# Last mixing of a four-layer spectral kernel in units of a quarter of the rows, round the four column groups

## Chip, cores and metric

One core of a Trainium2 chip runs the whole program. The metric is the device time of one execution in microseconds.

## What is computed

The input x is 16 images of 32 channels, 64 by 64, in float32. Four layers follow each other, each of the form x + layer(group norm of x). The change concerns the fourth, a full spectral convolution, and the place where its weights' spectra are made and kept:

```python
def _L3_conv_ref(x, weights):              # weights: (32, 32, 64, 64)
    x_f = jnp.fft.rfft2(x)
    k_f = jnp.fft.rfft2(weights)
    out_f = jnp.einsum('bchw,ochw->bohw', x_f, k_f)
    return jnp.fft.irfft2(out_f, s=(H, W))
```

For each frequency the einsum mixes 32 input channels into 32 output channels: a complex 32x32 product applied to 16 images.

## The kernel before

`kernel_spectra_stage` runs first. For each of 8 tiles of the fourth layer's weights, PE transposes and multiplies (L378 to L417), DVE and ACT empty the banks, and ACT gathers the spectra of a tile in `ks_spec` (L352, eight copies) and stores them with two DMAs from its own queue (L357) in the DRAM tensor `kf`. Before the first copy of the next tile, ACT waits until they have landed (`stored`). The other layers follow. The first one has a mixing of its own (`l0_mix_stage`, L762): 448 matmuls with 64 rows by 32 weight columns and 32 moving columns, whose neighbours lie in different column groups and alternate between two halves of the rows; it is not in a hardware loop. In the second layer, L1048 and L1082 are a subtraction (on POOL and DVE in turn) and a cast on DVE.

In the fourth layer the forward transform leaves the spectrum of x in `xm`: 128 partitions are four groups of 32 channels, one group for each quarter of the frequencies of a slot; the free axis is slot (8), frequency (64), real or imaginary, image (16). `l3_mix_stage` multiplies by the weights' spectra and writes the result back over `xm`, and `inverse_stage` (L840 on) goes back to pixels and adds.

A complex product is one real matmul here. Its contraction axis has 128 rows: for two slots (`s2`) 32 real and 32 imaginary channels each. The stationary side are 128x32 of `m_kf`, the moving side 64 columns of `m_xp`. For these, three copies on DVE stage each quadrant of 32 partitions: the spectrum as it is into the real rows (L1513), and into the imaginary rows the real part (L1514) and the negated imaginary part (L1515), the turned spectrum. A result of 32 rows lies in one of the four column groups of a bank. A float32 matmul stands as two records in the trace.

The order of the work is written out by hand. The loops run over four pairs of slots `i`, two pairs of groups `p`, two halves of the frequencies `half`, the two groups `j` of the pair, and 32 frequencies `m`. So 32 matmuls in a row lie in the same column group (L1561); after 64, `mixed` is raised. DVE stages the next half but one as soon as `mixed` frees its `m_xp`; SP loads the spectra of a pair of groups (2 MB, four DMAs of 512 KB in 8 KB runs, each to 32 partitions, L1475) as soon as `m_kf` is free; ACT empties four banks on 64 partitions (L1577) after each half. POOL only zeroes one of two `m_xp` at the start (L1542, L1543).

```python
for m in range(H):
    at = (2 * p + j) * C
    last = pe.matmul(ps[4 * half + m // 8][at:at + C, m % 8 * N:(m % 8 + 1) * N],
                     kf[p][:, j, :, H * half + m],
                     xp[half][:, j, m].rearrange("p s n -> p (s n)"), ...)
```

## Time and profile before

| | |
|---|---|
| device time, median of 3 runs | 1067.43 us (1066.34 to 1069.4) |
| span of the profiled execution | 1065.9 us |
| PE busy | 907.4 us (85%) |
| DVE, ACT, POOL busy | 663.4, 520.5, 122.4 us |
| mixing matmuls, L1561 | 116.5 us busy, 2048 records |
| granted PE clock, mean | 0.948 |

The span runs from the first to the last instruction of one profiled execution; that execution's own device time is not listed apart from the runs, whose lowest lies 0.4 us above the span and whose median 1.5 us. A group of the profile gives the busy time, the mean of one instruction, and the idle time in front of it with what ended it. Idle time of an engine that is waited for by nobody costs nothing.

### The profile page before, as it was taken

Reading aid. Unit: us, or ns where it says so; the run is one execution under the profiler, and the core shown is the slowest. Engines: PE = TensorE matmul, PEld = TensorE weight load, DVE = VectorE, ACT = ScalarE, POOL = GpSimd, SP = SyncE. Lnnn points to the kernel's source line nnn. Section 1 sums busy time; section 2 is a strip of 40 time slices with the busy share of each in tenths; the row PEclk is TensorE's granted clock in tenths of the full one; section 3 lists DMA queues with packets and bytes.
Section 4 is the critical chain, followed back from the end, with each engine's and each line's share of the span. In section 5 each row is a group of like instructions: output and inputs, shape, how many; then the busy total and the mean of one; then the engine's idle time right before and its main releaser. Section 6 shows DMA issues by size and latency. Waiting matters only on the chain. (4 is left out here: it accounts for less than half of the span.)

```text
span 1065.9 us, 25662 instructions
## 1 busy us (share of the span) xinstructions
PE 907.4 (85%) x9335; PEld 764.7 (72%) x9335; DVE 663.4 (62%) x1208; ACT 520.5 (49%) x900; POOL 122.4 (11%) x120
## 2 busy tenths in 40 slices
PE   6999999876449956599789999995888699998998
PEld 6999999765348843499644444443887699998998
DVE  3556463765584769578778565756666688881232
ACT  2444444575344436255369997000888423225554
POOL 0000000010001016155401223000000100001110
PEclk9999999898679989699999999997999899999999
DMA  6465766464300000000000000001300337750222
GB/s 249 159 243 195 272 216 202 129 147 94 76 4 1 0 14 1 0 1 0 0 2 1 0 0 0 0 0 29 66 0 0 79 82 146 145 103 1 89 108 118
DMA packets 47673, 79.12 MB, mean 74 GB/s; under 512 B 19322, under 2 KB 37888, under 8 KB 44816
## 3 DMA queue, kind: packets, MB, share of 16 engines
q1 hardware_dynamic: 30992, 61.80, 20.9%
q10 hardware_dynamic: 16640, 16.78, 4.5%
q8 instruction: 26, 0.43, 0.2%
q14 instruction: 15, 0.12, 0.0%
HBM read 50.65 MB, written 27.92 MB: 74 GB/s over the span
## 5 line engine op out<-in xcount | busy, mean ns | idle before, releaser
L1436 DVE SCALAR_TENSOR_TENSOR X<-bank,c_power,X 32x512 f32 x128 | 95.8, 748 | 58.8 <-PE bank L1404 53.6
L1561 PE MATMUL bank<-m_xp,m_kf 128*32 128x64 f32 x2048 | 116.5, 224 | 6.8 <-DVE m_xp L1529 5.4
L1561 PEld LDWEIGHTS bank<-m_xp,m_kf 128*32 128x32 f32 x2048 | 116.2, 139 | 7.2 <-issue 7.2
L1404 PE MATMUL bank<-c_rh,c_w_high 128*128 x288 | 110.3, 383 | 3.3 <-DVE c_rl L1349 3.3
L1404 PE MATMUL bank<-c_rl,c_w_high 128*128 x288 | 110.2, 383 | 0.0
L1404 PE MATMUL bank<-c_rh,c_w_low 128*128 x288 | 110.2, 383 | 0.0
L923 DVE TENSOR_TENSOR X<-X,bank 128x512 f32 x64 | 43.6, 682 | 91.6 <-PE bank L909 91.6
L204 DVE BATCH_NORM_STATS2 bn<-X 128x6 f32 x128 | 85.6, 684 | 2.4 <-POOL X L1208 1.6
L1577 ACT COPY xm<-bank 64x512 f32 x64 | 32.5, 584 | 95.4 <-PE bank L1561 95.4
L1363 ACT ACTIVATE c_r<-X,c_nrm 32x1024 f32 (+1 forms) x56 | 73.6, 1314 | 2.4 <-DVE c_nrm L1412 1.1
L438 DVE COPY ks_cols<-bank 128x512 f32<-128x512 f32 x64 | 42.6, 682 | 45.9 <-PE bank L404 45.9
L435 DVE COPY ks_tt<-bank 128x512 f32<-128x512 f32 x64 | 42.3, 688 | 44.1 <-PE bank L378 44.1
L352 ACT COPY ks_spec<-bank 128x512 f32<-128x512 f32 x64 | 37.4, 587 | 65.4 <-PE bank L412 29.1
L1161 PE MATMUL bank<-mm,p_tt 128*128 128x128 f32 x512 | 63.0, 278 | 3.1 <-DVE X L1191 3.1
L385 PE MATMUL bank<-ks_fw,ks_tt 128*128 128x128 f32 x512 | 64.6, 277 | 0.0
L412 PE MATMUL bank<-ks_fh,ks_cols 128*128 128x128 f32 x512 | 63.7, 275 | 0.0
L1161 PEld LDWEIGHTS bank<-mm,p_tt 128*128 128x128 f32 x512 | 59.9, 193 | 4.8 <-DVE X L1191 4.5
L385 PEld LDWEIGHTS bank<-ks_fw,ks_tt 128*128 128x128 f32 x512 | 61.3, 194 | 0.0
L447 ACT COPY ks_src<-bank 128x512 f32<-128x512 f32 x64 | 37.2, 587 | 48.4 <-PE bank L385 48.4
L412 PEld LDWEIGHTS bank<-ks_fh,ks_cols 128*128 128x128 f32 x512 | 60.4, 192 | 0.0
L909 PE MATMUL bank<-c_l_iw,i_tt 128*128 128x128 f32 (+1 forms) x384 | 60.1, 310 | 0.0
L626 DVE TENSOR_TENSOR f_tl<-bank,f_th 128x512 f16<-128x512 f32 x64 | 42.3, 683 | 26.1 <-ACT f_th L581 25.9
(187 smaller groups left out, 1951.7 us busy)
## 6 DMA issues: line engine op xcount, KB each, us to landing
ks_src<-in_L_conv_weights SPq DMA_DIRECT2D x32, 512.0 KB, 6.3
kf<-ks_spec ACTq DMA_DIRECT2D x16, 1024.0 KB, 10.0
m_kf<-kf SPq DMA_DIRECT2D x32, 512.0 KB, 8.0
X<-in_x SPq DMA_DIRECT2D x4, 2048.0 KB, 12.3
out_y<-X SPq DMA_DIRECT2D x16, 512.0 KB, 2.7
xf<-f_xm SPq DMA_DIRECT2D x6, 448.0 KB
l_wb<-in_L_conv_weights_r SPq DMA_DIRECT2D x4, 512.0 KB, 13.1
l_wb<-in_L_conv_weights_i SPq DMA_DIRECT2D x4, 512.0 KB, 14.7
```

The source lines that it names most:

```text
L204: dve.bn_stats(self.bn[:, c, :], self.X[:, q, c * CH:(c + 1) * CH]).then_inc(step, 1)
L385: m = pe.matmul(ps[4 + j % 4][:, k * P:(k + 1) * P], tt[j % 4][:, k * P:(k + 1) * P], fw[:], start=True, stop=True)
L412: m = pe.matmul(ps[4 + s % 4][:, b * P:(b + 1) * P], cols[:, b, 4 * s:4 * s + 4].rearrange("p s c -> p (s c)"), fh[:], start=True, stop=True)
L435: dve.tensor_copy(tt[j % 4][:], ps[j % 4][:]).then_inc(turned_read, 1)
L438: dve.tensor_copy(cols[:, :, 4 * s:4 * s + 4].rearrange("p b s c -> p s b c"), ps[s % 4][:].rearrange("p (s b c) -> p s b c", s=4, b=IB)). ...
L909: m = pe.matmul(ps[4 + c % 4][:, k * n:(k + 1) * n], tt[g % 4][:, (first + k) * P:(first + k + 1) * P], mw[:], start=True, stop=True)
L923: dve.tensor_tensor(x, x, ps[4 + c % 4][:], ALU.add).then_inc(added, 1)
L1161: m = pe.matmul(ps[2 + 2 * (j % 2) + t][:, k * P:(k + 1) * P], tt[j % 2][:, k * P:(k + 1) * P], mm[:, t, :], start=True, stop=True)
L1363: act.activation(to, of, ACT.Identity, scale=nrm[at, 0, bass.ds(q, 1)], bias=nrm[at, 1, bass.ds(q, 1)]).then_inc(ready[b], 1)
L1404: m = pe.matmul(ps[n][:], w[:, ky, kx].rearrange("p o c -> p (o c)"), d[:, q, b, y:y + HALF, x:x + HN], start=i == 0, stop=i == len(terms) ...
L1436: dve.scalar_tensor_tensor(x, ps[n][o * C:(o + 1) * C, :].rearrange("p (y x) -> p y x", x=HN), filt.power[at, 2:3], x, ALU.mult, ALU.add). ...
L1561: last = pe.matmul(ps[4 * half + m // 8][at:at + C, m % 8 * N:(m % 8 + 1) * N], kf[p][:, j, :, H * half + m], xp[half][:, j, m].rearrange( ...
```

## The change

The mixing goes in four units of 16 frequencies a pair of slots, and within a unit through all four column groups for each frequency. `m_xp` holds four groups of 16 frequencies instead of two of 32. The spectra of the weights lie in DRAM by halves of the frequencies, so that one load brings all four groups of one half: as before 2 MB, in runs of 4 KB; the stores of a tile become four DMAs with runs of 512 bytes. Staging is divided: POOL writes the turned spectrum of a unit, for all 128 partitions at once, into a new tile `m_turned` (one subtraction from zero, one copy); DVE copies the eight quadrants of the spectrum and three of the turned one into `m_xp`, ACT the other five. ACT empties two banks on 128 partitions a unit, one unit behind its staging. PE waits for both stagers (`staged`), POOL for both before it writes over `m_turned`, the stagers for `swapped` of POOL and for `mixed` of two units before. In the first pair, where the real frequencies at the edge are packed, small extras of POOL and DVE replace the fix-up copies.

```diff
-        self.kf = nc.dram_tensor("kf", (SLOT // 4, P, 2, C // IB, IB * N), F32, kind="Internal").ap()
+        self.kf = nc.dram_tensor("kf", (SLOT // 4, P, 2, 2, C // IB, IB * HN), F32, kind="Internal").ap()
...
-        spec = pr.sb(ctx, "ks_spec", [P, SLOT // 4, 2, IB, N])
+        spec = pr.sb(ctx, "ks_spec", [P, SLOT // 4, 2, 2, IB, HN])
...
                             if s == 0:
-                                act.wait_ge(stored, START + 64 * i + 32 * p)
-                            act.copy(spec[:, s].rearrange("p r o k -> p o r k"),
-                                     ps[4 + s % 4][:].rearrange("p (o r k) -> p o r k", o=IB, r=2)
+                                act.wait_ge(stored, START + 128 * i + 64 * p)
+                            act.copy(spec[:, s].rearrange("p r h o k -> p o (r h) k"),
+                                     ps[4 + s % 4][:].rearrange("p (o r k) -> p o r k", o=IB, r=4)
                                      ).then_inc(made_read, 1)
                         act.wait_ge(made_read, START + base + 16)
-                        for part in range(2):
-                            act.dma_start(pr.kf[:, :, part, 2 * i + p, :].rearrange("s p n -> p s n"),
-                                          spec[:, :, part].rearrange("p s o k -> p s (o k)")).then_inc(stored, 16)
+                        for part, half in np.ndindex(2, 2):
+                            act.dma_start(pr.kf[:, :, part, half, 2 * i + p, :].rearrange("s p n -> p s n"),
+                                          spec[:, :, part, half].rearrange("p s o k -> p s (o k)")).then_inc(stored, 16)
...
-def load_kernel_spectra(sp, pr, to, i, pair, loaded):
+def load_kernel_spectra(sp, pr, to, i, half, loaded):
     for s2 in range(2):
         for part in range(2):
             at = (2 * s2 + part) * C
-            sp.dma_start(to[at:at + C].rearrange("c j o k -> c j (o k)"),
-                         pr.kf[2 * i + s2, pair * 2 * C:(pair + 1) * 2 * C, part].rearrange(
-                             "(j c) t n -> c j (t n)", j=2)).then_inc(loaded, 16)
+            sp.dma_start(to[at:at + C].rearrange("c g o k -> c g (o k)"),
+                         pr.kf[2 * i + s2, :, part, half].rearrange("(g c) t n -> c g (t n)", g=4)).then_inc(loaded, 16)
...
-    staged, mixed, mixed_read, fix, zeroed = (pr.sem(f"m3_{n}") for n in
-                                              ("staged", "mixed", "mixed_read", "fix", "zeroed"))
-    H = N // 2
+    UNITS = 4
+    H, U = N // 2, N // 4
+    staged = {n: pr.sem(f"m3_staged_{n}") for n in ("dve", "act")}
+    mixed, mixed_read, fix, zeroed, cleared, swapped = (pr.sem(f"m3_{n}") for n in
+                                               ("mixed", "mixed_read", "fix", "zeroed", "cleared", "swapped"))
     with ExitStack() as ctx:
-        kf = [kf0, pr.sb(ctx, "m3_kf1", [P, 2, C, N])]
-        xp = [pr.sb(ctx, f"m3_xp{p}", [P, 2, H, 2, 2 * B]) for p in range(2)]
+        kf = [kf0, pr.sb(ctx, "m3_kf1", [P, 4, C, H])]
+        xp = [pr.sb(ctx, f"m3_xp{p}", [P, 4, U, 2, 2 * B]) for p in range(2)]
+        turned = [pr.sb(ctx, f"m3_turned{p}", [P, 2, U, 2 * B]) for p in range(2)]
+        nought = pr.zero[:].unsqueeze(2).unsqueeze(3).broadcast_to([P, 2, U, B])
+        def spectrum(i, u):
+            return xm[:, bass.ds(2 * i, 2), U * u:U * u + U]
+        def copy_real(copy, i, u, only):
+            for g, s2 in only:
+                last = copy(xp[u % 2][2 * s2 * C:(2 * s2 + 1) * C, g, :, s2],
+                            xm[g * C:(g + 1) * C, 2 * i + s2, U * u:U * u + U].rearrange("p k r b -> p k (r b)"))
+            return last
+        def copy_imaginary(copy, u, only):
+            for g, s2 in only:
+                last = copy(xp[u % 2][(2 * s2 + 1) * C:(2 * s2 + 2) * C, g, :, s2],
+                            turned[u % 2][g * C:(g + 1) * C, s2])
+            return last
+        quadrants = [(g, s2) for g in range(4) for s2 in range(2)]
         with nc.Block() as block:
             @block.sync
             def _(sp):
                 load_kernel_spectra(sp, pr, kf[1], 0, 1, loaded[1])
                 with sp.Fori(1, PAIRS) as i:
-                    for p in range(2):
-                        sp.wait_ge(mixed, START + 4 * i + 2 * p - 2)
-                        load_kernel_spectra(sp, pr, kf[p], i, p, loaded[p])
-            def stage(dve, i, p, half, quadrants=(0, 1)):
-                for j in quadrants:
-                    for s2 in range(2):
-                        of = xm[(2 * p + j) * C:(2 * p + j + 1) * C, 2 * i + s2, H * half:H * half + H]
-                        re = xp[half][2 * s2 * C:(2 * s2 + 1) * C, j, :, s2]
-                        im = xp[half][(2 * s2 + 1) * C:(2 * s2 + 2) * C, j, :, s2]
-                        dve.tensor_copy(re, of.rearrange("p k r b -> p k (r b)"))
-                        dve.tensor_copy(im[:, :, B:2 * B], of[:, :, 0, :])
-                        last = dve.tensor_scalar(im[:, :, 0:B], of[:, :, 1, :], -1.0, None, ALU.mult)
-                return last
+                    for half in range(2):
+                        sp.wait_ge(mixed, START + UNITS * i + 2 * half - 2)
+                        load_kernel_spectra(sp, pr, kf[half], i, half, loaded[half])
+            @block.gpsimd
+            def _(pool):
+                pool.memset(xp[1][0:2 * C, :, :, 1], 0.0).then_inc(cleared, 1)
+                pool.memset(xp[1][2 * C:P, :, :, 0], 0.0).then_inc(cleared, 1)
+                pool.wait_ge(cleared, 2)
+                def turn(i, u, done):
+                    of, to = spectrum(i, u), turned[u % 2]
+                    pool.tensor_tensor(to[:, :, :, 0:B], nought, of[:, :, :, 1, :], ALU.subtract)
+                    pool.tensor_copy(to[:, :, :, B:2 * B], of[:, :, :, 0, :]).then_inc(done, 1)
+                for u in range(UNITS):
+                    if u >= 2:
+                        pool.wait_ge(staged["dve"], u - 1)
+                        pool.wait_ge(staged["act"], u - 1)
+                    turn(0, u, swapped if u % 2 else cleared)
+                    if u % 2 == 0:
+                        pool.wait_ge(cleared, u // 2 + 3)
+                        pool.memset(turned[0][0:C, 0, 0, 0:B], 0.0)
+                        pool.tensor_copy(turned[0][0:C, 0, 0, B:2 * B], xm[0:C, 0, U * u, 1, :]).then_inc(swapped, 1)
+                with pool.Fori(1, PAIRS) as i:
+                    for u in range(UNITS):
+                        pool.wait_ge(staged["dve"], UNITS * i + u - 1)
+                        pool.wait_ge(staged["act"], UNITS * i + u - 1)
+                        turn(i, u, swapped)
             @block.vector
             def _(dve):
-                for half in range(2):
-                    if half == 1:
-                        dve.memset(xp[1][0:2 * C, :, :, 1], 0.0)
-                        dve.memset(xp[1][2 * C:P, :, :, 0], 0.0)
-                    stage(dve, 0, 0, half, (0,)).then_inc(fix, 1)
-                    dve.wait_ge(fix, 3 * half + 1)
-                    dve.memset(xp[half][0:C, 0, 0, 0, B:2 * B], 0.0).then_inc(fix, 1)
-                    dve.memset(xp[half][C:2 * C, 0, 0, 0, 0:B], 0.0).then_inc(fix, 1)
-                    dve.tensor_copy(xp[half][C:2 * C, 0, 0, 0, B:2 * B], xm[0:C, 0, H * half, 1, :]).then_inc(staged, 1)
-                    stage(dve, 0, 0, half, (1,)).then_inc(staged, 1)
-                for half in range(2):
-                    dve.wait_ge(mixed, START + half + 1)
-                    stage(dve, 0, 1, half).then_inc(staged, 2)
+                dve.memset(xp[0][0:2 * C, :, :, 1], 0.0).then_inc(zeroed, 1)
+                dve.memset(xp[0][2 * C:P, :, :, 0], 0.0).then_inc(zeroed, 1)
+                dve.wait_ge(zeroed, 2)
+                dve.wait_ge(cleared, 2)
+                def stage(i, u, first=False):
+                    last = copy_real(dve.tensor_copy, i, u, quadrants)
+                    if first and u % 2 == 0:
+                        last.then_inc(fix, 1)
+                        dve.wait_ge(fix, u // 2 + 1)
+                        dve.memset(xp[0][0:C, 0, 0, 0, B:2 * B], 0.0)
+                    dve.wait_ge(swapped, UNITS * i + u + 1)
+                    copy_imaginary(dve.tensor_copy, u, quadrants[5:]).then_inc(staged["dve"], 1)
+                for u in range(UNITS):
+                    if u >= 2:
+                        dve.wait_ge(mixed, START + u - 1)
+                    stage(0, u, True)
                 with dve.Fori(1, PAIRS) as i:
-                    for p in range(2):
-                        for half in range(2):
-                            dve.wait_ge(mixed, START + 4 * i + 2 * p + half - 1)
-                            stage(dve, i, p, half).then_inc(staged, 2)
-            @block.gpsimd
-            def _(pool):
-                pool.memset(xp[0][0:2 * C, :, :, 1], 0.0).then_inc(zeroed, 1)
-                pool.memset(xp[0][2 * C:P, :, :, 0], 0.0).then_inc(zeroed, 1)
+                    for u in range(UNITS):
+                        dve.wait_ge(mixed, START + UNITS * i + u - 1)
+                        stage(i, u)
             @block.tensor
             def _(pe):
                 pe.sem_inc(mixed, START)
                 pr.keep_warm(pe, 16)
-                pe.wait_ge(zeroed, 2)
                 with pe.Fori(0, PAIRS) as i:
-                    for p in range(2):
-                        pe.wait_ge(loaded[p], 64 * i + 64)
-                        for half in range(2):
-                            pe.wait_ge(mixed_read, START + 4 * i + 2 * p + half - 1)
-                            for j in range(2):
-                                pe.wait_ge(staged, 8 * i + 4 * p + 2 * half + j + 1)
-                                pe.sem_inc(pr.pace, 1)
-                                for m in range(H):
-                                    at = (2 * p + j) * C
-                                    last = pe.matmul(ps[4 * half + m // 8][at:at + C, m % 8 * N:(m % 8 + 1) * N],
-                                                     kf[p][:, j, :, H * half + m],
-                                                     xp[half][:, j, m].rearrange("p s n -> p (s n)"),
-                                                     start=True, stop=True)
-                            last.then_inc(mixed, 1)
+                    for u in range(UNITS):
+                        half = u // 2
+                        if u % 2 == 0:
+                            pe.wait_ge(loaded[half], 64 * i + 64)
+                        for n in ("dve", "act"):
+                            pe.wait_ge(staged[n], UNITS * i + u + 1)
+                        pe.wait_ge(mixed_read, START + UNITS * i + u - 3)
+                        pe.sem_inc(pr.pace, 1)
+                        for m in range(U):
+                            for g in range(4):
+                                last = pe.matmul(ps[2 * u + m // 8][g * C:(g + 1) * C, m % 8 * N:(m % 8 + 1) * N],
+                                                 kf[half][:, g, :, U * (u % 2) + m],
+                                                 xp[u % 2][:, g, m].rearrange("p s n -> p (s n)"),
+                                                 start=True, stop=True)
+                        last.then_inc(mixed, 1)
             @block.scalar
             def _(act):
                 act.sem_inc(mixed_read, START)
-                with act.Fori(0, PAIRS) as i:
-                    for p in range(2):
-                        for half in range(2):
-                            act.wait_ge(mixed, START + 4 * i + 2 * p + half + 1)
-                            for m in range(4):
-                                at = slice(p * 2 * C, (p + 1) * 2 * C)
-                                k = H * half + 8 * m
-                                c = act.copy(xm[at, bass.ds(2 * i, 2), k:k + 8].rearrange("p s k r b -> p k s (r b)"),
-                                             ps[4 * half + m][at, :].rearrange("p (k s n) -> p k s n", s=2, n=2 * B))
-                            c.then_inc(mixed_read, 1)
+                def read(i, u):
+                    act.wait_ge(mixed, START + UNITS * i + u + 1)
+                    for m in range(2):
+                        k = U * u + 8 * m
+                        c = act.copy(xm[:, bass.ds(2 * i, 2), k:k + 8].rearrange("p s k r b -> p k s (r b)"),
+                                     ps[2 * u + m][:].rearrange("p (k s n) -> p k s n", s=2, n=2 * B))
+                    c.then_inc(mixed_read, 1)
+                def stage(i, u):
+                    act.wait_ge(swapped, UNITS * i + u + 1)
+                    copy_imaginary(act.copy, u, quadrants[:5]).then_inc(staged["act"], 1)
+                act.wait_ge(zeroed, 2)
+                act.wait_ge(cleared, 2)
+                for u in range(UNITS):
+                    if u >= 2:
+                        act.wait_ge(mixed, START + u - 1)
+                    stage(0, u)
+                    if u:
+                        read(0, u - 1)
+                with act.Fori(1, PAIRS) as i:
+                    for u in range(UNITS):
+                        act.wait_ge(mixed, START + UNITS * i + u - 1)
+                        stage(i, u)
+                        if u:
+                            read(i, u - 1)
+                        else:
+                            read(i - 1, UNITS - 1)
+                read(PAIRS - 1, UNITS - 1)
...
-                kf0 = pr.sb(inner, "m3_kf0", [P, 2, C, N])
+                kf0 = pr.sb(inner, "m3_kf0", [P, 4, C, HN])
```

What this does to the order on PE. Before, in a pair of slots (the loop's first half):

```order
L1555 ISA
L1557 ISA
L1561 MATMUL bank<-m_xp,m_kf 32x64 x32
L1557 REGISTER_ALU
L1561 MATMUL bank<-m_xp,m_kf 32x64 x32
```

and now, one unit and the start of the next:

```order
L1596 ISA
L1598 REGISTER_ALU
L1602 MATMUL bank<-m_xp,m_kf 32x64 x64
L1596 REGISTER_ALU
L1598 REGISTER_ALU
L1602 MATMUL bank<-m_xp,m_kf 32x64 x64
```

The two waits for two groups of a half have become one for a whole unit; the number of matmuls between two `mixed` stays 64.

On DVE, a quadrant and a half of the loop before (a half has four such threes):

```order
L1513 ISA
L1513 COPY m_xp<-xm 32x32x32
L1514 COPY m_xp<-xm 32x32x16
L1515 ISA
L1515 TENSOR_SCALAR m_xp<-xm 32x32x16
```

and now the end of a unit's eight copies, its three of the turned spectrum, and the start of the next:

```order
L1509 ISA
L1509 COPY m_xp<-xm 32x16x32
L1574 REGISTER_ALU
L1516 COPY m_xp<-m_turned 32x16x32 x3
L1583 REGISTER_ALU
L1509 ISA
L1509 COPY m_xp<-xm 32x16x32
```

The strided pair of each quadrant is gone; what DVE does in their place needs POOL's result only for the last three copies. On POOL, where the loop did not exist, a unit is:

```order
L1541 ISA
L1541 TENSOR_TENSOR m_turned<-zero,xm 128x32x16
L1542 ISA
L1542 COPY m_turned<-xm 128x32x16
```

The stage had two memsets there; now each unit puts two instructions of 512 elements on POOL.

## Rows read from the trace of the kernel before

**Rows 1.** Groups by line, L3 mixing: busy, mean ns | idle before, releaser.

```profile
L1561 PE MATMUL bank<-m_xp,m_kf 128*32 128x64 f32 x2048 | 116.5, 224 | 6.8 <-DVE m_xp L1529 5.4 <-DVE m_xp L1515 1.4
L1513 DVE COPY m_xp<-xm 32x1024 f32 (+1 forms) x64 | 45.4, 709 | 19.1 <-PE bank L1561 15.2 <-PEq L1449 3.1
L1577 ACT COPY xm<-bank 64x512 f32 x64 | 32.5, 584 | 95.4 <-PE bank L1561 95.4
L1514 DVE COPY m_xp<-xm 32x512 f32 (+1 forms) x64 | 28.5, 445 | 0.9
```

**Rows 2.** Timeline of the mixing: start us, us, engine, line, instruction.

```profile
903.69 0.68 DVE L1513 COPY m_xp<-xm 32x1024 f32 x1 [1.18 <-PE bank L1561]
904.38 0.42 DVE L1514 COPY m_xp<-xm 32x512 f32 x1
904.73 0.41 DVE L1515 TENSOR_SCALAR m_xp<-xm 32x512 f32 x1
905.15 0.69 DVE L1513 COPY m_xp<-xm 32x1024 f32 x1
...
910.73 0.68 DVE L1513 COPY m_xp<-xm 32x1024 f32 x1 [1.19 <-PE bank L1561]
...
969.70 2.77 DVE L840 COPY i_yq<-xm 128x512 f32<-128x512 f32 x8 [10.63 <-PEq L1496]
```

**Rows 3.** Windows in the L0 mixing: busy (x) of five engines, PEclk, DMA share, GB/s.

```profile
289.50:293.00 3.50, 3.50 (x207) 3.50 (x208) 3.39 (x8) 0.00 (x0) 0.00 (x0) 0.50 0.02 5
294.50:296.80 2.30, 2.30 (x128) 2.26 (x128) 2.27 (x7) 1.61 (x5) 0.00 (x0) 1.00 0.03 7
307.00:309.00 2.00, 1.55 (x93) 1.42 (x86) 1.92 (x6) 1.05 (x4) 0.00 (x0) 0.64 0.03 8
```

**Rows 4.** Timeline, start of the mixing, POOL beside DVE.

```profile
841.68 1.80 POOL L1542 MEMSET m_xp<- 64x2048 f32 x1 [177.15 <-POOLq L1449]
841.72 2.30 DVE L1513 COPY m_xp<-xm 32x1024 f32<-32x1024 f32 x1 [3.09 <-PEq L1449]
...
843.54 2.23 POOL L1543 MEMSET m_xp<- 64x2048 f32 x1
844.04 2.01 DVE L1514 COPY m_xp<-xm 32x512 f32<-32x512 f32 x1
```

**Rows 5.** Timeline, L1 stage, POOL subtracting beside DVE casts.

```profile
393.75 0.43 DVE L1082 CAST e_high_part<-e_src 128x512 f32 x1
...
395.10 1.40 POOL L1048 TENSOR_TENSOR e_low_part<-e_src,e_high_part 128x512 f32 x1 [39.53 <-DVE e_high_part L1082]
395.39 1.72 DVE L1082 CAST e_high_part<-e_src 128x512 f32 x2
```

**Rows 6.** Groups by line, other stages: prices of POOL and ACT instructions.

```profile
L1208 POOL TENSOR_TENSOR X<-X,p_tmp 128x512 f32 x32 | 40.5, 1272 | 57.3 <-DVE X L1191 57.3
...
L265 ACT ACTIVATE e_src<-X,shift,rstd 128x512 f32 x32 | 24.4, 806 | 8.8 <-DVE e_low_part L1048 3.7 <-DVEq L1070 3.6 <-POOL e_low_part L1048 1.6
...
L840 POOL COPY i_yq<-xm 128x512 f32 x24 | 13.6, 616 | 169.5 <-PE bank L866 169.5
```

**Rows 7.** DMA in 885:892 (m_kf), 210:218 (L0 weights), 41:44 (store), shares.

```profile
DMA packets 224, 1.44 MB, mean 206 GB/s; under 512 B 48, under 2 KB 48, under 8 KB 48
q1 hardware_dynamic: 224, 1.44, 101.0%
DMA packets 144, 1.57 MB, mean 197 GB/s; under 512 B 48, under 2 KB 48, under 8 KB 48
DMA packets 1144, 1.15 MB, mean 385 GB/s; under 512 B 17, under 2 KB 1144, under 8 KB 1144
q10 hardware_dynamic: 1144, 1.15, 108.3%
```

**Rows 8.** Timeline, kernel spectra, seventh tile: the wait for the store.

```profile
169.59 1.56 ACT L352 COPY ks_spec<-bank 128x512 f32<-128x512 f32 x3 [6.34 <-DMA kf<-ks_spec]
```

**Rows 9.** Window at the start of the inverse stage, columns as in rows 3.

```profile
970.00:972.00 2.00, 1.73 (x8) 1.76 (x9) 2.00 (x7) 0.59 (x1) 0.00 (x0) 0.50 0.02 4
```

6 lines of the change are left out of this document (3 added, 3 removed).

## The prediction

> **What bounds the kernel now.** I read the page first, then the groups by line, then the timeline of the last mixing, then the windows, the DMA view and the waits. In the groups the mixing matmuls of L1561 are busy 116.5 us, all but 6.8 of it without a gap, while ACT L1577 waits 95.4 us for them [rows 1]. So in this stage PE ends last. The timeline gives the beat. DVE begins to stage a half at 903.69 and the next at 910.73: 7.04 us for 64 matmuls (128 records), 55 ns a record, DVE 5.9 us of it [rows 2]. Sixteen such halves and their start fill 841.7 to 969.7, where the first copy of the inverse stage starts [rows 2, 4]: 128 us, the only stretch that the change reorders.
>
> **PE's term.** The matmul keeps its size (128x32 weights, 64 moving columns) and its number, 1,024. What is new is that neighbours lie in different column groups. The program already has a place that does this, L762, with 64 rows and 32 columns. At half clock it ran 207 records in 3.5 us, 17 ns each, at full clock 128 in 2.3 us, 18 ns [rows 3]. By columns alone, from 55 ns for 64, one after another, they would take 27 ns at full clock and 55 at half. So neighbours do run beside each other, and the pace that stays does not depend on the clock. I take 18 ns: 128 records of a unit in 2.3 us at full clock; at half clock the four groups' own 110 ns a record leave 27 ns, 3.5 us. Bounds: 1.8 us (a quarter of 7.04) and 7.04 (nothing gained). Either way but the last, PE stops being the bound and the stagers take over.
>
> **DVE's term.** A unit needs 8 copies of the spectrum and 3 of the turned one, each 32x512; before it was 4 of 1,024 and 8 of 512 elements a half. One of these last takes 0.42 and 0.41 us. The distance between starts is what counts: L1514 is followed after 0.35 us, L1515 after 0.42 [rows 2], though the mean of L1514, with its first in it, reads 445 ns [rows 1]. L1514 and L1515 write the same 32 partitions; from L1515 to L1513 they change, as they do at nearly every copy of the new order. So 11 x 0.43 = 4.7 us (lower bound 11 x 0.35 = 3.9). The Trainium skill, VectorE: DVE Perf Modes, section "Two Vector instructions with no wait between them", says that an instruction whose start quadrant differs from that of the one before it starts only when that has finished; the three distances agree.
>
> **POOL's term, and what it costs DVE.** POOL now turns each unit: one subtraction and one copy, 128x512. L1208 prices the first at 1.27, L840 the second at 0.62 [rows 6]: 1.9 us, well under a unit. But the first DVE copy of this stage took 2.30 us beside POOL's memset and the next 2.01 beside the second, against 0.69 and 0.42 later [rows 4, 2]. And where POOL subtracts (1.40 us), two DVE casts take 1.72 us, one alone 0.43 [rows 5]; two alone at L1514's distance take 0.78, so DVE lost 0.94 to a POOL instruction of 1.40. I book 0.94 for the subtraction and 0.3 for the copy (same share, rounded down): 4.7 + 1.2 = **6.0 us a unit**. Bounds: nothing lost, 4.7; all 1.9 lost, 6.6. The Trainium skill, SBUF — State Buffer, section "SBUF: two separate sides", makes the pair of ports that DVE and GpSimd share an exclusive lock for the full instruction; taken to the letter that is the 6.6 case, a rival below.
>
> **ACT and DMA beside it.** ACT has five copies out of SBUF at 0.81 or less (L265, 128x512 [rows 6]) and two bank reads at 0.58 [rows 1]: 5.2 us at most. It fits under 6.0, since read(u-1) comes behind stage(u) and PE's result of u-1 is there by then. Loads: 2 MB for every two units, at 206 GB/s [rows 7] 10.2 us, 5.1 a unit, with start 5.3. That floor is new; it was 5.1 under 7.04. The runs become 4 KB for 8 KB. The weights of L0, in 16 KB runs to 32 partitions as well, moved at 197 GB/s, so it is bytes and not runs that cost [rows 7]; I book nothing. What covers a slower load is the 0.7 us between 5.3 and 6.0.
>
> **Start and tail.** DVE's two memsets, 1.8 each like POOL's first [rows 4], with gaps 4.2 us; then one unit with POOL's two small extras, 6.6. The first unit is staged at 841.7 + 10.8 = 852.5. That is later than now, because a whole unit must be ready and both halves of the zeroing come first. Fifteen units at 6.0: 942.5. Last unit on PE 2.3 to 3.5, say 3.0, two reads 1.1, out of the block 0.4: 947.0 against 969.7, **22.7 us saved**. In pair 0 PE also meets its code for the first time; L762, which is in no loop, is not busy throughout its windows either (1.55 of 2.00 us [rows 3]). Under 6.0 us a unit such pauses are covered. If the cover goes, it costs about 1.5 us for each of four units.
>
> **What is given back.** PE will be busy 2.3 of 6.0 us. In the L0 mixing, with bursts and pauses, the granted clock dropped from 1.00 to 0.64 within 307 to 309 [rows 3]. Half clock in the mixing is hidden (3.5 under 6.0), but the inverse stage may start in it. It starts at 0.50 already now [rows 9]; I book 1.5 us more for a longer stretch. Bounds 0 and 4.
>
> **The store.** Each tile of the kernel spectra is stored in 512-byte runs, four issues for two. Runs of 1 KB: 1,144 packets in 3 us at 108.3% of 16 engines, 45 ns each [rows 7]. At 512 B between half of that and all: 4,096 packets take 5.8 to 11.6 us, 5.8 now. ACT reads into the same tile a good 14 us after the issue. Its longest wait for them lasts 6.34 us, until 169.59, and then it runs three copies without a pause [rows 8]; PE has four banks of slack before it feels that. I book 0.5 us, bounds 0 and 8. Two more issues cost ACT about 1 us a tile, ahead of row copies with the same slack: nothing.
>
> **Sum.** 22.7 - 1.5 - 0.5 = 20.7 us less than the profiled span of 1065.9. The median of the runs, 1067.43, lies 1.5 above that span, the lowest 0.4. On the median: **1046.7 us**.
>
> **Rivals.**
> - *POOL costs DVE little* (0.15). For it: in the casts part of POOL's time was no loss. Then the loads bound: 15 x 5.3 saves 10.5 us more, about 1036.
> - *POOL shuts DVE out entirely* (0.12). 4.7 + 1.9 = 6.6 a unit: 9.9 back, with the start 0.6, about 1057. For it: the memset rows, where DVE lost all 1.6 us. It is also what the SBUF page's rule would give.
> - *The column groups do not overlap at 128 rows* (0.07); the change then does not do what it says. L762 alternates between two row halves, so each partition feeds two of four neighbours; four from all 128 rows is not shown. PE stays at 7.04: 852.5 + 16 x 7.04 + 1.5 = 966.6, 3 us saved, 0.5 given back, about 1065.
> - *Slower: the kernel-spectrum loads* (0.06). If a packet of 4 KB costs what one of 8 KB costs (at 101.0% of 16 engines in 7 us and 224 packets, 48 of them small, 16 x 7 x 1.01 / 176 = 0.64 us), a load takes 512 x 0.64 / 16 = 20.5 us. Seven follow each other from about 843, the last ready at 986.5; two units, a read and the exit on top, 993: 23 us longer, with clock and store about 1092. It decides from (969.7 - 6.5 - 843) / 7 = 17 us a load, 0.54 us a packet. Against it: L0's weights.
>
> **How the numbers follow.** Forecast 0.60, rivals 0.15, 0.12, 0.07, 0.06. The measurement can tell about 0.3%, 3.2 us, from no change. Faster: 0.60 + 0.15 + 0.12 + 0.02 of the third rival, 0.89; same 0.05; slower 0.06. The range runs from 1035 (loads bound) to 1060 (all of POOL lost and the clock's 4 us); it leaves out the last two.
>
> **What would show it.** Right: units 6.0 us apart, DVE without waits on PE, ACT waiting for PE or POOL, unit matmuls in 2.3 or 3.5 us, single DVE copies of 1 us and over beside POOL. POOL's subtraction at 1.27 to 1.5. First bank read near 856, inverse stage at 947. Wrong: PE never idle (third rival), PE waiting for m_kf (loads), ACT's first L352 of a tile waiting over 10 us or PE L412 behind it (store), DVE copies at 0.43 throughout (first rival).

## The result, and the profile after

| | before | changed |
|---|---|---|
| device time, median of 4 runs each | 1068.41 us (1066.34 to 1070.67) | 1083.2 us (1079.89 to 1084.14) |
| ratio, 95% interval | | 1.0131 [1.0107, 1.0155] |
| span of the profiled execution | 1065.9 us | 1082.1 us |
| granted PE clock, mean | 0.948 | 0.920 |

Slower by 1.3%, where 2% faster was forecast. The mixing gained nearly what was forecast, and the time was lost elsewhere. The groups by line of the changed kernel, against [rows 1]:

```profile
L1509 DVE COPY m_xp<-xm 32x512 f32 (+1 forms) x128 | 69.8, 545 | 6.4 <-PE bank L1602 4.5
L1602 PE MATMUL bank<-m_xp,m_kf 128*32 128x64 f32 x2048 | 54.8, 280 | 48.3 <-DVE m_xp L1516 37.8 <-issue 6.8 <-DMA m_kf<-kf 3.5
L1516 ACT COPY m_xp<-m_turned 32x512 f32<-32x512 f32 x80 | 50.1, 626 | 7.6 <-POOL m_turned L1553 6.5
L1541 POOL TENSOR_TENSOR m_turned<-zero,xm 128x512 f32<-128x512 f32 x16 | 18.5, 1159 | 58.5 <-DVE m_xp L1516 58.4
```

The mixing matmuls are busy 54.8 us instead of 116.5, and PE now waits for DVE. The timeline of the same stage, the answer to [rows 2] and [rows 4], DVE's first instruction, then PE's rows, then DVE's first of the inverse stage:

```profile
879.43 1.76 DVE L1562 MEMSET m_xp<- 64x2048 f32 x1 [3.55 <-PEq L1449]
```

```profile
890.44 4.01 PE L1602 MATMUL bank<-m_xp,m_kf 128*32 128x64 f32 x128 [9.38 <-DVE m_xp L1516]
...
902.37 3.03 PE L1602 MATMUL bank<-m_xp,m_kf 128*32 128x64 f32 x123 [2.27 <-DVE m_xp L1516]
911.84 4.25 PE L1602 MATMUL bank<-m_xp,m_kf 128*32 128x64 f32 x133 [6.44 <-issue]
...
929.91 3.13 PE L1602 MATMUL bank<-m_xp,m_kf 128*32 128x64 f32 x128 [3.47 <-DMA m_kf<-kf]
935.12 3.67 PE L1602 MATMUL bank<-m_xp,m_kf 128*32 128x64 f32 x128 [2.08 <-DVE m_xp L1516]
941.01 3.52 PE L1602 MATMUL bank<-m_xp,m_kf 128*32 128x64 f32 x128 [2.22 <-DVE m_xp L1516]
946.87 3.68 PE L1602 MATMUL bank<-m_xp,m_kf 128*32 128x64 f32 x128 [2.33 <-DVE m_xp L1516]
```

```profile
985.67 2.77 DVE L840 COPY i_yq<-xm 128x512 f32<-128x512 f32 x8 [4.87 <-PEq L1522]
```

From 935 on the starts lie 5.87 us apart. From POOL's first memset at 878.93 to 985.67 the stage lasts 106.7 us, where [rows 2, 4] gave 128.0: 21.3 us saved.

So 37 us were lost before it (878.93 against 841.68). The first matmul of L199 is the first work of the layers behind the kernel spectra; it starts at 205.1 us in the kernel before and at 241.6 us in the changed one, **36.5 us later**. The stages between it and the mixing take nearly the same time in both (638.3 us to the last L199 before, 639.2 after). ACT's and PE's timeline in the first two tiles of the kernel spectra, after the change:

```profile
35.06 6.87 ACTq L357 DMA_DIRECT2D kf<-ks_spec  x4
42.04 2.54 ACT L447 COPY ks_src<-bank 128x512 f32<-128x512 f32 x5 [7.16 <-issue]
...
60.15 11.66 ACTq L357 DMA_DIRECT2D kf<-ks_spec  x4
72.26 1.28 ACT L447 ACT_TABLE_LOAD   x1 [12.28 <-issue]
```

```profile
65.82 0.60 PE L378 MATMUL bank<-ident,ks_src 128*128 128x128 f32 x4
74.19 5.88 PE L385 MATMUL bank<-ks_fw,ks_tt 128*128 128x128 f32 x32 [7.77 <-ACT ks_src L447]
```

The four DMA issues of a tile's store take ACT 6.87 us in the first tile and 11.66 us in the second; in the kernel before the second tile's two took 1.03. Behind them in ACT's order stand the copies of L447 that empty PE's banks for the next tile. PE fills its banks, stops at 66.4 and stands until 74.19. The waits of the stage, ACT's and PE's, summed:

```profile
ACT L447 <- issue: 35.9, 3, 12.3
...
PE bank L385 <- ACT ks_src L447: 25.7, 6, 7.8
```

Tiles that were 23.5 us apart are now 25 and 33 us apart in turn; only the last gap still is 23.5. The long ones are those beside SP's 2 MB load of X. The short ones up to the sixth tile have a load of weights beside them (queue q1, 1.65 MB between 34 and 55 us); the last two tiles have no load, and there the four issues take this:

```profile
209.64 3.94 ACTq L357 DMA_DIRECT2D kf<-ks_spec  x4
```

The issues one by one, as min/median/max in ns, are best read in two windows, the first tile (no load of X beside it) and the second (with it). Here for the kernel before, both tiles in one window, 35 to 59 us:

```profile
L357 ACTq DMA_DIRECT2D kf<-ks_spec x4: 379/455/487, 35.4 to 59.4; - x4
```

and for the changed one, a window for each tile:

```profile
L357 ACTq DMA_DIRECT2D kf<-ks_spec x4: 436/933/4084, 35.1 to 40.5; - x4
...
L357 ACTq DMA_DIRECT2D kf<-ks_spec x4: 378/1646/7524, 60.2 to 69.0; - x4
```

In order the first tile's four took 436, 468, 4084 and 1398 ns: the first two as before, the third and fourth not.

### The profile page after: what moved, and what is told of

The parts are those of the page before. It is cut to its first block and busy times, and to the rows that moved or that the text cites. A ratio compares the mean times of both kernels' runs of the same rounds, so it can differ in the third digit from the quotient of the medians.

```text
span 1082.1 us, 25800 instructions
## 1 busy us (share of the span) xinstructions
PE 854.3 (79%) x9335; PEld 706.8 (65%) x9335; DVE 657.4 (61%) x1188; ACT 553.5 (51%) x948; POOL 153.0 (14%) x156
## 5 line engine op out<-in xcount | busy, mean ns | idle before, releaser
L1602 PE MATMUL bank<-m_xp,m_kf 128*32 128x64 f32 x2048 | 54.8, 280 | 48.3 <-DVE m_xp L1516 37.8
L385 PE MATMUL bank<-ks_fw,ks_tt 128*128 128x128 f32 x512 | 71.6, 296 | 25.7 <-ACT ks_src L447 25.7
L1602 PEld LDWEIGHTS bank<-m_xp,m_kf 128*32 128x32 f32 x2048 | 51.9, 189 | 51.3 <-issue 51.3
L385 PEld LDWEIGHTS bank<-ks_fw,ks_tt 128*128 128x128 f32 x512 | 67.6, 211 | 27.1 <-ACT ks_src L447 27.1
L1509 DVE COPY m_xp<-xm 32x512 f32 (+1 forms) x128 | 69.8, 545 | 6.4 <-PE bank L1602 4.5
L352 ACT COPY ks_spec<-bank 128x512 f32<-128x512 f32 x64 | 37.6, 587 | 65.2 <-PE bank L417 32.9
L447 ACT COPY ks_src<-bank 128x512 f32<-128x512 f32 x64 | 35.3, 593 | 52.8 <-PE bank L385 45.6
## 6 DMA issues: line engine op xcount, KB each, us to landing
X<-in_x SPq DMA_DIRECT2D x4, 2048.0 KB, 11.7
```

The source lines that it names most:

```text
L385: m = pe.matmul(ps[4 + j % 4][:, k * P:(k + 1) * P], tt[j % 4][:, k * P:(k + 1) * P], fw[:], start=True, stop=True)
L1509: last = copy(xp[u % 2][2 * s2 * C:(2 * s2 + 1) * C, g, :, s2], xm[g * C:(g + 1) * C, 2 * i + s2, U * u:U * u + U].rearrange("p k r b -> p ...
L1602: last = pe.matmul(ps[2 * u + m // 8][g * C:(g + 1) * C, m % 8 * N:(m % 8 + 1) * N], kf[half][:, g, :, U * (u % 2) + m], xp[u % 2][:, g, m ...
```

## The experiments

All are compared with the kernel before, measured on the same chip (its medians there 1067.45, 1069.24 and 1069.28 us). Ratios are to it. Letters name theories, as the expectations do.

### The kernel before, its store cut into four

Nothing of the change, only four issues for two; the runs stay at 1 KB, so the bytes and the packets are those of before.

```diff
-                        for part in range(2):
-                            act.dma_start(pr.kf[:, :, part, 2 * i + p, :].rearrange("s p n -> p s n"),
-                                          spec[:, :, part].rearrange("p s o k -> p s (o k)")).then_inc(stored, 16)
+                        for part, sh in np.ndindex(2, 2):
+                            act.dma_start(
+                                pr.kf[sh * 4:sh * 4 + 4, :, part, 2 * i + p, :].rearrange("s p n -> p s n"),
+                                spec[:, sh * 4:sh * 4 + 4, part].rearrange("p s o k -> p s (o k)")).then_inc(stored, 16)
```

> The kernel before, with each tile's store cut into four issues instead of two: 1 KB runs as before, half the slots each, so 2,048 descriptors a tile as before. Theory Q (ACT is held in a DMA issue while more than some 2,000 descriptors of its queue are under way): no issue of L357 over 1 us, time as before, 1068 within 3 us. Rival N (a queue takes only two large DMAs at a time, whatever their number of descriptors): the third and fourth issue are held 3 to 8 us and the kernel loses 30 to 37 us, 1098 to 1105. Rival S (the time goes to the slower store itself, 512-byte packets beside the loads of X): as before, 1068.

1091.28 us, 1.0223 [1.0192, 1.0253], outside the range of every theory. The cut into four issues alone makes the kernel slower; the packets are the same in number and size. The second tile, issues of 512 descriptors (one to a run) each:

```profile
L357 ACTq DMA_DIRECT2D kf<-ks_spec x4: 378/524/5776, 57.3 to 59.2; - x4
```

The first tile's took 442, 393, 1055 and 1062 ns. Total descriptors (2,048) are as before, where nothing was held: Q is false as put. N, "every issue beyond the second", is nearer, but the third took 1.06 us in the first tile and 0.55 in the second, where only the fourth, with 1,536 descriptors ahead, was held.

### The kernel before, 512-byte runs in four issues

The cut by `oh` (two of the four blocks of a row a DMA) instead of by slots: 4,096 descriptors, the mixing untouched.

```diff
-                        for part in range(2):
+                        for part, oh in np.ndindex(2, 2):
+                            act.dma_start(
+                                pr.kf[:, :, part, 2 * i + p, oh * 2 * N:(oh + 1) * 2 * N].rearrange("s p n -> p s n"),
+                                spec[:, :, part, oh * 2:oh * 2 + 2].rearrange("p s o k -> p s (o k)")).then_inc(stored, 16)
```

> The kernel before, mixing untouched, with the store in four issues of 512-byte runs (each of two of a tile's four output channels), 4,096 descriptors a tile. All three theories put the loss in the kernel spectra: Q and N expect the third and fourth issue held (4 to 8 and 2 to 3 us) and the loss of the changed kernel, 34 to 38 us: 1102 to 1106. S expects the same loss with no ACT row copy late behind an issue. If it is below 1080 the loss came with the mixing after all.

1103.32 us, 1.0328 [1.0292, 1.0364]; L199 starts at 240.2, 35 us later than before. The loss of the change appears in full with its store alone, and in the mixing there is none to look for. Its two tiles on ACT's timeline:

```profile
34.28 6.79 ACTq L357 DMA_DIRECT2D kf<-ks_spec  x4
...
59.29 11.50 ACTq L357 DMA_DIRECT2D kf<-ks_spec  x4
```

### The changed kernel, its store on SP's queue

The same four DMAs of 512-byte runs, issued by SP behind the weight loads of the tile two on; the load of X follows them.

```diff
+                def store(t):
+                    sp.wait_ge(made_read, START + 16 * t + 16)
+                    for part, half in np.ndindex(2, 2):
+                        sp.dma_start(pr.kf[:, :, part, half, t, :].rearrange("s p n -> p s n"),
+                                     spec[:, :, part, half].rearrange("p s o k -> p s (o k)")).then_inc(stored, 16)
...
+                with sp.Fori(1, tiles // 2) as i:
+                    for p in range(2):
+                        load(i, p)
+                        store(2 * i + p - 2)
+                    load_x(i)
```

> The changed kernel, with the same four store DMAs a tile issued by SP's queue instead of ACT's (4,096 descriptors as in the changed kernel), each behind the weight load of two tiles on, and ahead of the load of X. Q and N: the issues are held on SP, where nothing is queued that is soon needed; ACT's row copies follow the last spectra copy at once, the kernel spectra take what they took before plus 0 to 4 us, and the 21 us of the mixing come through: 1047 to 1052. S: the store is as slow as in the changed kernel and the next tile's first L352 waits for it: 1070 or more.

1048.04 us, 0.9802 [0.9769, 0.9834], as Q and N expected; S fell. SP is held now, and nothing that is soon needed stands behind it:

```profile
34.94 6.75 SPq L310 DMA_DIRECT2D kf<-ks_spec  x4
...
58.42 6.43 SPq L310 DMA_DIRECT2D kf<-ks_spec  x4
```

L199 starts at 207.7, 2.5 us later than before. The transfers themselves, then, were as harmless as forecast; holding the engine that issues them was not.

### Eight issues a tile on ACT, spread

Four after the fourth slot, four after the eighth.

```diff
-                        act.wait_ge(made_read, START + base + 16)
-                        for part, half in np.ndindex(2, 2):
-                            act.dma_start(pr.kf[:, :, part, half, 2 * i + p, :].rearrange("s p n -> p s n"),
...
+                            if s % 4 == 3:
+                                act.wait_ge(made_read, START + base + NCH + s + 1)
+                                for part, half in np.ndindex(2, 2):
+                                    act.dma_start(
...
```

> The changed kernel, with the store on ACT's queue in eight issues a tile: four after slot 3 (2,048 descriptors), four after slot 7. Q: after slot 3 there is room; after slot 7 part of the first 2,048 has gone, and the issues are held for some 2 to 4 us in tiles without the load of X, more in those with it; much of it under the slack of four banks: 1050 to 1065. N: each tile holds six of eight issues, worse than the changed kernel: 1085 to 1110. S: near the changed kernel, 1075 to 1083.

1087.28 us, 1.0179 [1.0147, 1.0212]. Q missed again in its time, and N's time came without its mechanism: the first four issues, 2,048 descriptors in all, passed, and the second four were held. The second tile:

```profile
58.77 3.13 ACTq L358 DMA_DIRECT2D kf<-ks_spec  x4
64.21 10.43 ACTq L358 DMA_DIRECT2D kf<-ks_spec  x4
```

The second four, which find the first four not yet moved, take more than three times as long as those. So neither a fixed number of issues nor the tile's total of descriptors is the rule.

### One issue a tile

`kf` and `ks_spec` get the real and imaginary part and the half outside the slot, so that all of a tile's 4,096 runs of 512 bytes are one DMA.

```diff
-        self.kf = nc.dram_tensor("kf", (SLOT // 4, P, 2, 2, C // IB, IB * HN), F32, kind="Internal").ap()
+        self.kf = nc.dram_tensor("kf", (P, 2, 2, SLOT // 4, C // IB, IB * HN), F32, kind="Internal").ap()
...
-                        for part, half in np.ndindex(2, 2):
-                            act.dma_start(pr.kf[:, :, part, half, 2 * i + p, :].rearrange("s p n -> p s n"),
-                                          spec[:, :, part, half].rearrange("p s o k -> p s (o k)")).then_inc(stored, 16)
+                        act.dma_start(pr.kf[:, :, :, :, 2 * i + p, :].rearrange("p r h s n -> p (r h s) n"),
+                                      spec[:].rearrange("p r h s o k -> p (r h s) (o k)")).then_inc(stored, 16)
```

> The changed kernel with the tiles kf and ks_spec laid out so that a tile's whole store is one DMA of 4,096 descriptors of 512 bytes, issued by ACT. Theory G (a queue holds the issuing engine only from the third issue that is still waiting for its descriptors on; how long depends on their number): no hold of a second or more, kernel spectra as before, 1045 to 1052. Rival R (the room is a number of descriptors, some 2,048, whatever the issues): the one instruction is held itself, 4 us and over in tiles without the load of X and 7 and over with it, 1060 to 1083.

**1044.54 us**, 0.9773 [0.974, 0.9805], the fastest of the complete kernels here. All eight issues of the kernel:

```profile
L356 ACTq DMA_DIRECT2D kf<-ks_spec x8: 548/549/673, 34.8 to 199.4; - x8
```

4,096 descriptors in one issue take ACT 0.55 us: G's forecast, while R fell, which would have had the one issue held for 4 us and more. L199 starts at 204.7, 0.4 us earlier than before. ACT's wait for the store, of which [rows 8] is one, comes to this in the whole stage:

```profile
ACT ks_spec L352 <- DMA kf<-ks_spec: 18.2, 3, 8.1
```

Three waits, 8.1 us at most, and the tiles stay 23.5 us apart: PE's banks cover them.

### Two issues a tile in the same layout, cut in three ways

As above with two DMAs: of 2,048 descriptors each, then of 1,024 and 3,072, then of 3,072 and 1,024.

```diff
-                        act.dma_start(pr.kf[:, :, :, :, 2 * i + p, :].rearrange("p r h s n -> p (r h s) n"),
-                                      spec[:].rearrange("p r h s o k -> p (r h s) (o k)")).then_inc(stored, 16)
+                        for lo, hi in ((0, 1), (1, 4)):
+                            act.dma_start(
+                                pr.kf.rearrange("p r h s t n -> p (r h) s t n")[:, lo:hi, :, 2 * i + p, :].rearrange(
+                                    "p q s n -> p (q s) n"),
+                                spec.rearrange("p r h s o k -> p (r h) s o k")[:, lo:hi].rearrange(
+                                    "p q s o k -> p (q s) (o k)")).then_inc(stored, 16)
```

> The same layout with two issues a tile of 2,048 descriptors each. G: neither is held, 1045 to 1052. R: the second is held, as long as the third and fourth of the changed kernel together or a little less, 1065 to 1083.

> As the run with two issues of 2,048 descriptors, same layout, but cut unevenly: first an issue of 1,024 descriptors of 512 bytes, right behind it one of 3,072. Theory A (an issue is held by the descriptors that its own queue has still to move, whatever its own size): 1,024 are ahead, as ahead of the second issue of the kernel before, which took 455 ns; so neither is held, both take 0.4 to 0.7 us, the tiles lie 23.5 us apart, and the run ends as the one with a single issue, 1,043 to 1,047 us. Theory S (an issue is held until those ahead and its own fit together into something like 3,000): 1,024 and 3,072 make 4,096 as in every cut of the same store, so the second is held 4 us and more, 9 beside the load of X, and the run takes 1,065 to 1,085 us.

> The same two issues in the other order: 3,072 descriptors, then 1,024. Theory A: 3,072 are ahead of the second, more than the 2,048 that held it 4.7 and 9.2 us in the run with two equal issues; about 1,000 more descriptors at 27 ns on 16 engines are 1.7 us more, so it is held 6 to 7 us, 10 to 12 beside the load of X, and the run takes 1,075 to 1,087 us, as the change itself. Theory S: the sum is the same in every cut, so held as in the run with equal issues, within 1 us of 4.7 and 9.2, and 1,069 to 1,076 us in all. Theory C (the second issue of 1,024 is short, so it passes as the fourth issue of the change did in 1.4 us): 1,045 to 1,055 us.

| ahead of the second issue | its own | held, first and second tile | time, ratio |
|---|---|---|---|
| 1,024 | 3,072 | 0.47, 0.65 us | 1049.7 us, 0.9804 [0.9769, 0.9839] |
| 2,048 | 2,048 | 4.7, 9.2 us | 1072.29 us, 1.0033 [1.0011, 1.0054] |
| 3,072 | 1,024 | 6.3, 11.0 us | 1085.14 us, 1.0156 [1.0127, 1.0186] |

The maximum of each row, in the second tile, is the second issue. Small one first:

```profile
L357 ACTq DMA_DIRECT2D kf<-ks_spec x2: 379/512/645, 59.2 to 59.8; - x2
```

Two equal ones:

```profile
L357 ACTq DMA_DIRECT2D kf<-ks_spec x2: 378/4778/9178, 58.7 to 59.3; - x2
```

Large one first:

```profile
L357 ACTq DMA_DIRECT2D kf<-ks_spec x2: 378/5701/11024, 58.9 to 59.4; - x2
```

The same bytes, and only the order of a small and a large issue decides over 35 us. Theory A gave both ends beforehand (no hold; 6 to 7 and 10 to 12); S and C fell, and so did G, which expected nothing of two equal issues. What holds an issue is what its queue still has ahead, not its own size. The traces also have each packet of the queue, so one can count how many of those ahead are still to move when the held issue goes in: 1,221 and 1,279 with two equal issues (first and second tile), 856 and 919 with the large one first; over all tiles and all issues that had at least 2,048 ahead in these two runs it was 856 to 1,854. So it does not wait for an empty queue, but until a good part of the backlog has moved. That also says why the fourth issue of the change took less than the third (1,398 against 4,084 ns): by then 1,064 of the 3,072 issued before it had moved.

The time of the small-first run misses A's range by 2.7 us in its median (its four runs go from 1044.77 to 1050.06, those of the one-issue kernel from 1043.86 to 1046.21). L199 starts at 205.6 there, 0.9 us later than with one issue. The rest of the 5.3 us between the two profiled executions lies in stages that the edit does not touch: 3.2 us between L199 and the mixing and 1.5 us from the inverse stage on. Other runs show the same differences there (table at the end of the experiments), so they do not speak about the store.

### The mixing: group after group

The kernel with SP's store, with the two loops of a unit's matmuls exchanged.

```diff
-                        for m in range(U):
-                            for g in range(4):
+                        for g in range(4):
+                            for m in range(U):
```

> The kernel with the store on SP's queue, with one thing turned round in the mixing: TensorE goes through all rows of a unit for one column group before it takes the next, as the kernel before did, instead of going round the four groups. Theory O (matmuls of different column groups overlap, which is why 128 records took 3.1 to 3.7 us in the change): the records take 55 ns each again, 128 of them 7.0 us, more than DVE's and POOL's 5.87 us a unit, so TensorE sets the unit: 15 units x 1.2 us more and about 1 us at the start, the mixing 120 to 127 us instead of 106.6, and 1,064 to 1,069 us in all. Rival P (what overlapped is due to the shorter units or the operands, not to the order): PE's unit stays below 4 us, units 5.9 us apart, 1,046 to 1,050 us.

1064.59 us, 0.9965 [0.9945, 0.9985], 16.6 us more than with the groups in turn, and all in the mixing (842.2 to 966.1, 123.9 us, against 106.6). In the window 894 to 935, columns as in [rows 3] with all five engines, groups one after another and then, in the changed kernel, in turn:

```profile
894.00:935.00 41.00, 40.92 (x792) 40.81 (x789) 28.60 (x70) 25.96 (x44) 9.55 (x12) 1.00 0.75 154
```

```profile
894.00:935.00 41.00, 20.24 (x773) 18.86 (x769) 35.44 (x73) 27.07 (x46) 11.48 (x12) 0.91 0.67 141
```

PE is busy for 40.92 us with 792 records, 52 ns each, against 20.24 us with 773, 26 ns each. The overlap of neighbours in different column groups is real, and it halves the time. It is most of the gain of the change: with it gone, a unit takes 6.7 us (1,024 records without a pause in 53.5 us), PE is the bound again, and of the 21.3 us saved in the mixing 4.1 are left. The second row also measures what is left: DVE busy 35.4 of 41 us with the 6.44 us stop in it.

### The mixing: POOL's turning left out

The kernel with SP's store; for pairs 1 to 3 POOL turns no spectrum (one tiny instruction keeps its place), so the product with the turned spectrum uses old data.

```diff
                     for u in range(UNITS):
                         pool.wait_ge(staged["dve"], UNITS * i + u - 1)
                         pool.wait_ge(staged["act"], UNITS * i + u - 1)
-                        turn(i, u, swapped)
+                        pool.tensor_tensor(turned[u % 2][:, 0:1, 0:1, 0:B], nought[:, 0:1, 0:1],
+                                           spectrum(i, u)[:, 0:1, 0:1, 1, :], ALU.subtract).then_inc(swapped, 1)
```

> The kernel with the stores on SP's queue, in which POOL's turning of the spectrum is left out for the pairs of slots 1 to 3 (it writes 16 elements instead, so the imaginary rows there are stale); waits and copies stay. Theory X (POOL's instruction shuts DVE's fast copies out): DVE takes 11 x 0.43 = 4.7 us a unit instead of 5.87 and the loads of 2 MB bound at 5.3; eleven units 0.57 faster or more, 6 to 9 us less than the kernel with stores on SP: 1039 to 1042. Rival (DVE's unit is long for another reason): units stay at 5.87, 1048.

1040.22 us, 0.9732 [0.9698, 0.9765], 7.8 us less than with it, inside X's range; the mixing itself takes 100.3 us instead of 106.6. Eight DVE copies take 3.43 us instead of 4.54, and PE then waits for the loads:

```profile
894.01 6.76 PE L1616 MATMUL bank<-m_xp,m_kf 128*32 128x64 f32 x256 [4.29 <-DMA m_kf<-kf]
904.25 3.11 PE L1616 MATMUL bank<-m_xp,m_kf 128*32 128x64 f32 x128 [3.48 <-DMA m_kf<-kf]
...
914.82 6.72 PE L1616 MATMUL bank<-m_xp,m_kf 128*32 128x64 f32 x256 [4.09 <-DMA m_kf<-kf]
```

Two units in 10.4 us, 5.2 each: the floor of the loads that the prediction had put at 5.3. DVE lost 1.1 us a unit beside POOL, but taking POOL away altogether brings only 0.7, because the loads then set the unit.

### The mixing: three quarters of its loads left out

The kernel with SP's store; kernel spectra are loaded for pair 0 alone and the other pairs use them.

```diff
-                with sp.Fori(1, PAIRS) as i:
-                    for half in range(2):
-                        sp.wait_ge(mixed, START + UNITS * i + 2 * half - 2)
-                        load_kernel_spectra(sp, pr, kf[half], i, half, loaded[half])
```

> The kernel with the stores on SP's queue, in which the loads of the weights' spectra for pairs 1 to 3 are left out (the products there use those of pair 0). Theory F (PE's stop of 6 us in the third unit is its next block of code, held up behind the 2 MB load): the stop goes and with it DVE's wait of 4.5 us; units stay 5.87 apart: 1042 to 1044. Rival (the stop is the fetch alone, whatever the DMA queues do): the time stays at 1048.

1044.32 us, 0.9768 [0.9733, 0.9803], 3.7 us less and 0.3 above F's range. The runs of the two kernels overlap (1042.84 to 1046.68, 1044.64 to 1051.76), so the times alone do not decide; the traces do: the mixing takes 103.5 us instead of 106.6. The stop in the third unit, 6.07 us with the loads (and 6.44 in the changed kernel), shrinks to this:

```profile
870.24 0.36 PE L1611 MATMUL bank<-m_xp,m_kf 128*32 128x64 f32 x5 [0.42 <-issue]
872.66 3.82 PE L1611 MATMUL bank<-m_xp,m_kf 128*32 128x64 f32 x128 [2.07 <-DVE m_xp L1529]
```

The stop carries "issue": no data were awaited. It falls where PE first meets this block of its code, and it is long only beside a 2 MB load. The fetch of the instructions stands in the traces as packets of 16 KB on queue q8. Without the loads one such packet starts 1.1 to 1.3 us after each of PE's first four units, the third here, in the window 867.8 to 868.9:

```profile
q8 instruction: 1, 0.02, 5.2%
```

In the changed kernel the first two come at 1.1 us as well. In the third unit, which starts at 902.37, none comes up to 908.9, while the load alone fills the 16 engines (first line, 902 to 908.9), and then it stands in the window 908.9 to 910.4 (second):

```profile
q1 hardware_dynamic: 403, 1.47, 101.5%
...
q8 instruction: 1, 0.02, 5.7%
```

It ends at 910.35, and PE goes on at 911.84, 1.5 us later; without the loads PE goes on 1.4 us after the packet's end. So PE's stop is the fetch, held up beside the load: theory F. That these packets are PE's is read from their times alone; the rows do not name the engine. The units stay 5.87 us apart without the loads, so in the steady part they cost nothing.

**The stages of all profiled executions.** Lengths in us: from the start to the first matmul of L199, from there to POOL's first instruction of the mixing, the mixing to the first copy of the inverse stage, and the rest.

| run | kernel spectra | layers between | last mixing | rest |
|---|---|---|---|---|
| before | 205.1 | 636.5 | 128.0 | 96.2 |
| changed | 241.6 | 637.3 | 106.7 | 96.4 |
| before, store cut into four | 222.1 | 639.7 | 127.9 | 96.5 |
| before, 512-byte runs in four issues | 240.2 | 637.1 | 128.0 | 96.1 |
| store on SP's queue | 207.7 | 639.2 | 106.6 | 96.5 |
| eight issues, spread | 245.9 | 635.8 | 106.2 | 96.4 |
| one issue | 204.7 | 636.3 | 106.9 | 94.9 |
| two equal issues | 229.4 | 639.4 | 107.1 | 94.9 |
| small one first | 205.6 | 639.4 | 106.7 | 96.4 |
| large one first | 242.9 | 636.6 | 106.9 | 96.4 |
| group after group | 206.7 | 635.5 | 123.9 | 96.4 |
| POOL's turning left out | 207.3 | 635.8 | 100.3 | 94.9 |
| loads left out | 207.4 | 636.0 | 103.5 | 96.5 |

The first and third columns move as the edits do. The second and fourth move by 4.2 and 1.6 us between kernels whose code there is the same; why is open, and a difference of that size in the total of one execution says nothing about an edit.

## Why the prediction was wrong

**The step that failed** is the last sentence of the store: "Two more issues cost ACT about 1 us a tile, ahead of row copies with the same slack: nothing." The four issues took ACT 6.9 and 11.7 us in the first two tiles, 6.5 to 11.4 in the next four and 3.9 in the last two, and what follows the kernel spectra began 36.5 us later. I had priced an issue by the instructions that stood in the trace, all of them issued into a queue with at most 1,024 descriptors ahead. The change puts 2,048 ahead of the third and, after its hold, still 2,008 ahead of the fourth (first tile). The bounds of 0 and 8 us came from packet time alone; no bound was made for the engine that issues. A bound could have been had from the same rows: an issue that cannot go in before the queue has moved what is ahead costs up to the transfer's length, the sum's own 5.8 us or more a tile, eight times, 46 us and more. Nor was the cover what I took it for. The slack of ACT's row copies before `ks_spec` is that of PE's banks; the issues stand ahead of the copies of L447, which empty the very banks that PE fills next. What I listed as a sign of this failure (ACT's first L352 waiting over 10 us) was the wrong wait as well: the sign was "issue" in front of L447.

**The rest of the store held.** Runs of 512 bytes: a tile's packets used 6.9 us of 16 engines against 5.9 (33.0% and 28.1% of 34 to 55 us), within 5.8 to 11.6, and with one issue the stage did not lengthen.

**The mixing held (21.3 us saved, 22.7 forecast), in part by terms that made up for each other.**

- *PE* was forecast at 18 ns a record, 27 at half clock. It took 24 at a granted clock of 1.00 (3.1 us for 128, at 964.49) and 29 at 0.54 (3.7 us, at 935.12). L762's 32 columns were a poor model for 64. It is hidden under DVE, as is the half clock.
- *DVE and POOL*: 6.0 us a unit forecast, 5.87 measured. Eight L1509 beside POOL take 4.54 us, 3.43 alone, so 1.1 us is lost; 1.2 was booked. The three turned copies take 1.29, 0.43 each, as taken. POOL's 1.16 and 0.80 us make 2.0: DVE lost somewhat more than half of it. One unit of the changed kernel, DVE's second and third copy and POOL's two instructions:

```profile
941.23 1.17 DVE L1509 COPY m_xp<-xm 32x512 f32 x1
942.41 0.75 DVE L1509 COPY m_xp<-xm 32x512 f32 x1
```

```profile
940.94 1.17 POOL L1541 TENSOR_TENSOR m_turned<-zero,xm 128x512 f32<-128x512 f32 x1 [3.92 <-DVE m_xp L1516]
942.06 0.82 POOL L1542 COPY m_turned<-xm 128x512 f32 x1
```

The six other copies take 0.42 each. The two long ones end 0.29 and 0.28 us after POOL's instruction (942.11 and 942.88), where a copy alone needs 0.42. POOL's two start 0.27 and 0.34 us before DVE's running copy ends; where DVE stands still, at 908.19, they take 1.04 and 0.61 us. The Trainium skill, SBUF — State Buffer, section "SBUF: two separate sides", has the one that starts first hold the shared ports for its whole instruction and the other wait. The trace agrees, but for some 0.14 us at each change. What was wrong in the 6.6 us is that DVE would lose all of POOL's time: POOL waits for DVE too, and that part costs DVE nothing. (That rival's 9.9 us is also a slip: 15 units of 0.6 and the start's 0.6 make 9.6.)

- *ACT*: copies out of SBUF at 0.63, not 0.81. It has room.
- *Loads*: a packet of 4 KB took 328 ns and one of 8 KB 648, so the slower rival, at the price of 8 KB for 4, was false. The slower result came by a mechanism that I had not listed.
- *Start*: 11.5 us to the first PE matmul, 10.8 forecast.
- *The stop at new code*: booked as covered, at 1.5 us if not. It was 6.44 us, of which DVE waited 4.47 for PE; the fifth unit starts at 917.47, 3.4 us behind the beat. With the 0.7 us of the start this is why the stage saved 21.3 instead of 22.7 us although the units were faster than forecast. PE's wait of 3.47 us for the loads, at 929.91, costs nothing: the next unit is on the beat again. With the loads left out the stop was 0.42 us and the mixing 3.1 us shorter.
- *Clock*: the granted clock is 1.00 in 984 to 986 and 0.61 in 986 to 988, as the inverse stage starts; before, it started at 0.50. From the stage's first copy to the end the kernel took 96.2 us before and 96.4 after, so of the 1.5 us booked 0.2 can be seen, less than these lengths differ from run to run.

**The sum without the failed step**: the kernel with one issue measured 1044.54 us against a forecast of 1046.7 for the change. That it is so near is in part luck: the terms above are off by 0.7 to 3.4 us each, in both directions, and the rest behind the mixing was 1.3 us shorter than before without a reason in the edit. Of the rivals, the one without overlap was false, but its price was right: with the groups one after another 1064.59 us were measured, about 1065 forecast.

## What to carry to other kernels

A DMA issue was cheap here only while its queue was short. Before splitting a transfer into more DMAs, count the descriptors (runs) that will stand ahead of each on its queue, and ask which engine issues them and what is behind that on its instruction stream: merge them into one DMA by the order of the dimensions in DRAM, put the small one first, or issue from an engine that nobody waits for. When a change rearranges one stage to help another, price the stage where the data are written with the same care as the one where they are read.
